# Table loads of the output stage issued on ScalarE's queue in a graph-network layer, one core

## The reference, cut to what matters

```python
h = jnp.maximum(_layernorm(x, axis=-1), 0.0)                      # x: 100000 x 64, float32
msgs_f = _mlp2(concat[h[src], h[dst], edge_attr], W1_f, b1_f, W2_f, b2_f)   # 25000 edges
agg = segment_sum(msgs_f, dst)
msgs_r = _mlp2(concat[h[dst], h[src], edge_attr], W1_r, b1_r, W2_r, b2_r)
agg = agg + segment_sum(msgs_r, src)
node_in = concat[agg, h]
return x + h + relu(node_in @ Wn1 + bn1) @ Wn2 + bn2              # 100000 x 64
```

## Time and profile before

| | |
|---|---|
| median of 3 runs | 1660.63 us (1658.93 to 1661.26) |
| the profiled execution | 1659.15 us, of which the span in the trace is 1657.4 us |
| begin stage | about 0 to 280 us |
| edge stage | about 280 to 1390 us; the last addition to the table lands before 1390.78 us |
| output stage | 1390.78 us, the first table load, to the end |
| issued in the output stage | 98 table loads of 512 KB, 98 stores and 53 loads of x + h of 256 KB |

### The profile page before, as it was taken

How to read it: one execution, slowest core, us unless ns; L and a number is a source line. 1 busy time by engine, 2 the same in 40 slices (tenths; PEclk the granted TensorE clock), 3 DMA queues, 4 the chain that set the end, 5 groups by cost and what they waited for, 6 DMA issues and landing times.

```text
span 1657.4 us, 28338 instructions
## 1 busy us (share of the span) xinstructions
PE 1317.6 (79%) x7070; PEld 997.1 (60%) x7070; DVE 963.5 (58%) x2913; ACT 945.1 (57%) x2256; POOL 1140.0 (69%) x963
## 2 busy tenths in 40 slices
PE   5898989777777777777878777777877783999998
PEld 4677777555555555555656565555665562666665
DVE  6899998655655555556555655565556550222222
ACT  4788888644444544444444445454544542777776
POOL 6999999788888888888888888888888763000000
PEclk9999999777777877777777778777777776999999
DMA  5999998455555555455545555555555545999998
GB/s 159 307 314 310 313 311 286 127 92 98 102 100 93 104 99 101 90 97 101 100 91 103 94 93 104 98 101 95 95 99 101 100 78 169 345 348 353 363 355 289
DMA packets 238362, 280.87 MB, mean 169 GB/s; under 512 B 53138, under 2 KB 155168, under 8 KB 238316
## 3 DMA queue, kind: packets, MB, share of 16 engines
q1 hardware_dynamic: 168012, 241.67, 44.2%
q0 software_dynamic: 68992, 38.59, 20.1%
q10 hardware_dynamic: 1312, 0.20, 0.1%
HBM read 162.62 MB, written 117.72 MB: 169 GB/s over the span
## 4 chain that ended last, share of the span: by engine, by line
POOL 40%; issue 29%; DMA 15%; DVE 11%; PE 2%; DVEq 1%; ACT 1%; SPq 1%; POOLq 1%; ACTq 0%
POOL table L540 31%; DMA out_x<-ncentred 11%; POOL got_ring L522 9%; DVE nvar L1074 4%; DVE ncentred L1068 2%; DMA table<-to_send,scatter_at 2%; DVE ncentred L1143 2%; DVE all_rstd L1078 1%; DVE all_sums L1061 1%; PE bank L875 1%; DVE nh L1085 1%; DMA same<-table 1%; DMA nx<-in_x 1%; PE bank L886 0%; DMA ends_int<-in_dst 0%
## 5 line engine op out<-in xcount | busy, mean ns | idle before, releaser
L540 POOL DMA_INDIRECT table<-to_send,scatter_at x392 | 644.7, 1645 | 141.1 <-issue 123.8
L850 PEld LDWEIGHTS bank<-message,same 128*128 128x128 f32 x1960 | 280.5, 230 | 44.4 <-issue 40.8
L850 PE MATMUL bank<-message,same 128*128 128x128 f32 x1960 | 301.7, 321 | 3.5 <-DVE message L1015 3.5
L651 ACT ACTIVATE nh<-nx,all_sums,all_rstd 128x64 f32<-128x64 f32 x784 | 280.5, 434 | 2.8 <-DMA nx<-in_x 2.8
L522 POOL DMA_INDIRECT got_ring<-in_x,gather_at x224 | 222.3, 992 | 68.3 <-issue 67.0
L812 PE MATMUL bank<-ident,h_ends 128*128 128x128 f32 x196 | 56.4, 385 | 241.1 <-DVE h_ends L1024 204.0
L782 PE MATMUL bank<-wn_h,nturned 128*128 128x256 f32 x784 | 197.3, 395 | 28.5 <-ACT nhidden L689 22.9
L1009 DVE TENSOR_TENSOR scatter_at<-moved,ids 128x4 int32<-128x4 f32 x98 | 16.0, 163 | 344.5 <-DMA table<-to_send,scatter_at 344.5
L522 POOL DMA_INDIRECT got_ahead<-in_x,gather_first x148 | 159.7, 1079 | 35.5 <-issue 23.7
L782 PEld LDWEIGHTS bank<-wn_h,nturned 128*128 128x128 f32 x784 | 143.5, 193 | 65.0 <-issue 32.2
L812 PEld LDWEIGHTS bank<-ident,h_ends 128*128 128x128 f32 x196 | 27.3, 185 | 256.3 <-issue 248.0
(11 more groups left out here) (78 smaller groups left out, 1974.3 us busy)
## 6 DMA issues: line engine op xcount, KB each, us to landing
nx<-in_x SPq DMA_DIRECT2D x194, 256.0 KB
table<-nhidden SPq DMA_DIRECT2D x97, 512.0 KB
same<-table SPq DMA_DIRECT2D x97, 512.0 KB, 5.4
others<-numbers SPq DMA_DIRECT2D x196, 128.0 KB
out_x<-ncentred SPq DMA_DIRECT2D x97, 256.0 KB, 4.1
nx<-out_x SPq DMA_DIRECT2D x55, 256.0 KB, 4.4
out_x<-nh SPq DMA_DIRECT2D x37, 256.0 KB
table<-to_send,scatter_at POOLq DMA_INDIRECT x392
```

Of the source, the lines that this page charges most:

```text
L540: pool.indirect_dma_start(table, bass.IndirectOffsetOnAxis(ap=scatter_at[s][:, k:k + 1], axis=0), to_send[s][:, k, :], None, compute_op=AL ...
L651: last = act.activation(nh[s][:, g, :], nx[place][:, g, :], ACT.Relu, bias=all_sums[:, at, g:g + 1].rearrange("p a g -> p (a g)"), scale=a ...
L850: last = pe.matmul(bank[6 + s][:, k * M:(k + 1) * M], same[s][:, o, k * P:(k + 1) * P], message[s][:, o, :], start=(o == k), stop=(o == KB ...
```

## The change

The table loads of the output stage leave SP's queue. ACT issues them, in its `window(w)` behind the two activations of relu_nodes(w) and ahead of add_bias(w - 1), for window w + NRING = w + 4. There is no wait of their own any more: relu_nodes(w) waits for `n_turned` of window w already, and that is the window whose place is loaded anew. Ahead of the stage ACT, and no more SP, waits for `s_added` and issues the first four loads (before, SP issued three there and the fourth in its pass 0). SP keeps the stores and the loads of x + h. ACT's loop ends at window 92 where it ended at 96.

```diff
@@ sync
-            def load_table(i, s, turn, place):
-                if not first(turn):
-                    sp.wait_ge(n_turned[s], 2 * (i - 1))
-                load_window(table[0:N, :], i, s, ntab[place], n_tab[place])
...
-            for s in range(2):
-                sp.wait_ge(s_added[s], 16 * KB * PAIRS)
-            for k in range(3):
-                Step(NW, 0).do(load_table, k, ring=NRING)
-
             def window(w):
-                w.do(load_table, 3, ring=NRING)
                 w.do(store, -2)
                 load_xh(w, -2)
@@ scalar
+            def load_table(i, s, turn, place):
+                w = 2 * i + s
+                if isinstance(i, int) and w == NW - 1:
+                    act.dma_start(ntab[place][0:LASTP, :], table[w * WIN:N, :].rearrange("(p g) m -> p (g m)", g=G)
+                                  ).then_inc(n_tab[place], 16)
+                else:
+                    act.dma_start(ntab[place], table[bass.ds(w * WIN, WIN), :].rearrange("(p g) m -> p (g m)", g=G)
+                                  ).then_inc(n_tab[place], 16)
+
+            for s in range(2):
+                act.wait_ge(s_added[s], 16 * KB * PAIRS)
+            for k in range(NRING):
+                Step(NW, 0).do(load_table, k, ring=NRING)
+
             def window(w):
                 w.do(relu_nodes)
+                w.do(load_table, NRING, ring=NRING)
                 w.do(add_bias, -1)
 
-            run(act, NW, [(4, 96, 4)], 1, window)
+            run(act, NW, [(4, 92, 4)], 1, window)
```

## The result

The changed kernel is **slower**: 1675.12 us median of 13 runs (1664.99 to 1678.17) against 1658.52 us of the kernel before, also 13 runs. The ratio is 1.0094, with a 95% interval of 1.0077 to 1.011, some 16 us. The forecast was 1652.6 us, and its range ended at 1668.

The account below looks back on a forecast made before the run. The prediction took late stores holding back table loads, and so PE, as the output stage's bound. Pitch 2.624 to 2.54 us over 95 windows saved 8.0 us, ACT's cost 0: median 1660.63 to 1652.6 us, range 1647.5 to 1668.

Parts of the forecast that it names:

- What bounds the kernel now: Output stage: the chain of stores and DVE additions holds back table loads, so PE stalls; whole prize 10.9 us.
- Loads leave SP, loads come earlier: SP's queue: 98 issues gone, worth nothing by themselves; loads some 1.5 to 3.5 us earlier, ending 9.2 us of PE stalls.
- What it adds on ACT: ACT in the output stage: one DMA issue per window, 0.54 us, hidden beside the relus, cost 0.
- Rival D: ACT: the DMA issue is not hidden and delays add_bias; 10 us more, 1671 us; chance 0.10.
- (a) Bytes: DMA engines in the output stage: 364 GB/s taken as the rate, which sets a pitch of 2.54 us per window.
- Rival B: DMA engines give no more than 357 GB/s: pitch 2.588, 3.4 us saved, 1657.2 us; chance 0.14.
- (b) The store loop: Output stage, DVE addition, hand-over and store: landing falls from 4.4 to 3.7 us, the loop to 2.25 us per window.
- Rival C: Store loop stays: pitch 2.62, PE's wait moves from table load to DVE's bank, 1660.6 us plus or minus 2; chance 0.18.
- Rival E: Table loads in the second queue crowd out stores, landing 4.9 us: 21 us more, 1681 us; chance 0.08.

Follow-up runs that it names:

- e2: Kernel before with four output tiles in place of two, all table loads still on SP: 1649.53 us, ratio 0.9922.
- e3: Kernel before with table loads still on SP but issued four windows ahead, in front of store w - 2: 1662.69 us, ratio 1.0001.
- e1: Changed kernel with four output tiles in place of two: 1652.65 us, ratio to the kernel before 0.9936.
- e8: Kernel before without the output stage's x + h loads, two output tiles, table loads on SP: 1647.88 us, 7 runs.
- e14: Changed kernel without x + h loads, four output tiles, ACT issuing the table load four ahead and behind add_bias: 1649.59 us, one run.
- e9: Changed kernel without the output stage's x + h loads and with four output tiles: 1649.06 us, one run.
- e11: Kernel before without x + h loads, four output tiles, table loads on SP four ahead, 1.2 us before the next store: 1644.21 us, one run.
- e5: Changed kernel with each table load cut in two DMAs of 2 KB per partition, packets of 2048 bytes: 1672.94 us, ratio 1.0097.
- e13: Changed kernel with one line moved, ACT issuing the load of w + 4 behind add_bias(w - 1): 1677.67 us, ratio 1.0096.

## Why the prediction was wrong, point by point

- *What bounds the kernel now*: right. The store loop was read off the chain and the waits, and e2 confirms both it and the prize: 2.504 us of pitch against the 2.509 read from rows 3, and a ratio of 0.9922, 13 us (9 to 17 by its interval), where 10.9 us were worked out.
- *Loads leave SP, loads come earlier*: right and without worth. PE's waits for table loads are gone, and e3, which does that alone, changes nothing. The stalls for loads were a symptom of late stores. (The stage's start, which was to stay, took 2.6 us more: the first load went out 1.3 us later and windows 0 and 1 took 1.3 us more; why is not shown.)
- *What it adds on ACT*: right, 0. Rival D is refuted by the timeline after, and by e1.
- *(a) Bytes*: the caution was needless. 364 GB/s was taken; e1 and e2 sustain 374 and 371, at pitches of 2.51 and 2.50 us. Rival B is refuted.
- ***(b) The store loop*: the step that failed.** It had the right form of loop, and had the change of the landing wrong, in sign too: half of a 512 KB load was to vanish from in front of the store, for 3.7 us in place of 4.4. Measured were 4.7 us for stores, where it had been 4.2, and 2.796 us of pitch in place of 2.54; the 0.36 us by which the mean landing grew, shared by two windows, turn 8 us of gain into 16 of loss. The step treated the load only as something ahead in a queue, that a queue of its own takes away. SP's order put a load right behind each store too (rows 7: store, x + h, table load), and e8 and e14 show that there one queue kept the load from delaying the store and two did not; and e9 shows that a load ahead of a store in another queue delays it as one in the same queue does (e11). So no load left the store's way. Which of the two made the 0.5 us of the full kernel stays open. That the formula met the pitch before exactly was luck: its 4.4 us were the median of stores and loads of x + h together, and with the stores' own 4.2 it gives (0.69 + 0.15 + 4.2) / 2 = 2.52 us, by their mean 2.59.
- *Rival C*, the wait moves from the table load to DVE's bank and the time stays: that is what e3 does, without the second queue. *Rival E*, stores at 4.9 us and 1681 us, was the case nearest to what came true, at 4.7 us and 1675; that the second queue takes more than its part, its reason, is not shown. It had 0.08. The rows gave it more: pitch depended on half the landing time, the landing stood, as it was read, 0.2 us over its threshold, and no row bore on two queues at all, so both signs of the change in landing should have stood near to each other, and the range should have reached to the pitch of 3.1 named as the bound.
- The Trainium skill (DMA: Bandwidth & Descriptors, Queues, rings and completion order) was quoted for turns packet by packet. Its packet is a bundle, typically of some 9 to 17 descriptors. e5 halved the smaller units of 4096 bytes that the profile calls packets, and the delay of the stores stayed (4.6 us), so e5 speaks against turns by that unit and doesn't test the page's rule. The same page's "Issuing engines are not separate DMA queues" says that a second issuing engine only saves sequencer time. For the rate e1 agrees (374 GB/s against 371 with one queue); for the time to land e14 does not, with its last parts landing 1.1 us later than in e8.

## What to carry to other kernels

Where a chain of waits runs through DMA landings, count the buffers in the loop before moving anything: pitch = (work + hand-over + landing) / number of buffers. If that is the measured pitch, one more pair of buffers is the cure (e2, e1), and an earlier or rearranged prefetch only moves the wait (e3). In one queue, program order can act as a priority: in e8 the loads issued behind a store left it nearly alone, and in e14, with a queue of their own, they did not. A load issued ahead of the store delayed it in either (e11, e9). Look at where the transfers go out in the trace, not in the program: e13 moved the line and not the load.

## What the runs showed of the hardware

- A 256 KB store landed in 3.3 us beside 512 KB loads issued behind it in the same queue, and in 4.8 us beside the same loads in another queue, at the same 313 GB/s (e8, e14; 3.4 and 4.5 us over all stores). In e14 it is the last parts that are late: the 8th of 16 landed at 2.2 us.
- With the load issued 1.2 us ahead of the store, it landed in 4.4 us in one queue and in 4.5 us in two (e11, e9).
- One core sustained 374 GB/s of mixed loads and stores over 220 us (e1), above the 358 GB/s per core that the Trainium skill gives (DMA: Bandwidth & Descriptors, Specifications), which is there half of what a memory stack has for two cores.
- ACT's sequencer issued a DMA, 0.34 us, beside a pair of activations without lengthening it: 1.27 us for the pair with and without it.
